# A quantised cross-attention and mixture-of-experts kernel on one core: a new instruction order for its front, and small jobs moved between VectorE, ScalarE and GpSimd

## The reference, cut to what matters

```python
# x (2, 512, 1024) f32, ctx_4096 (2, 1024, 1024) f32; all scales are 8/255, all zero points 128
def fake_quant(x, scale, zp):
    q = clip(round(x / scale + zp), 0, 255)
    return (q - zp) * scale

def xattn(x1, x2):                      # quantised product of normed tokens with the context
    return matmul(fake_quant(x1, s1, z1), fake_quant(x2, s2, z2))

def ffn(xt):                            # 1024 tokens
    scores = softmax(xt @ router_w + router_b) + router_bias
    # best 2 of 4 groups of experts, then best 2 of the 16 experts; their scores gate them
    for e in range(16):                 # here two experts are in use
        h = silu(xt @ ew1[e] + eb1[e]) * (xt @ ew2[e] + eb2[e])
        y += gate[:, e, None] * (h @ ew3[e] + eb3[e])
    z = silu(xt @ sw1 + sb1) * (xt @ sw2 + sb2) @ sw3 + sb3      # shared expert, 512 wide
    return y + z

x = x + tanh(g_xattn) * xattn(layernorm(x), ctx_4096)
x = x + tanh(g_ffn) * ffn(layernorm(x))
```

## Time and profile before

| what | value |
|---|---|
| device time, 3 runs | 317.53, 317.70, 319.18 us; median 317.7 |
| the profiled execution | 317.24 us, of which the profiler's span is 315.4 us |
| TensorE busy | 302.6 us, 96% of the span |
| VectorE busy | 206.3 us, 65% |
| ScalarE busy | 115.0 us, 36% |
| GpSimd busy | 13.9 us, 4% |
| granted TensorE clock | 0.998 of full speed |

### The profile page before, as it was taken

One profiled execution on the slowest core, in us unless ns is written; L12 is line 12 of the kernel. 1 busy time (PEld: TensorE's weight loads), 2 busy tenths in 40 slices (PEclk: granted clock), 3 DMA queues, 4 the chain that ended last, 5 costly groups with the idle time before them and its releaser, 6 DMA issues.

```text
span 315.4 us, 4716 instructions
## 1 busy us (share of the span) xinstructions
PE 302.6 (96%) x1867; PEld 153.3 (49%) x1867; DVE 206.3 (65%) x346; ACT 115.0 (36%) x129; POOL 13.9 (4%) x27
## 2 busy tenths in 40 slices
PE   4899899999999999999999999999999999999993
PEld 4653499644444446444444444444444444444441
DVE  3888999999998967776464361748564306135543
ACT  2877689589633559211108000064000000111000
POOL 2100120100002110000000000000000000000000
PEclk9999999999999999999999999999999999999999
DMA  7999908447620547105800008400000000000355
GB/s 234 410 337 321 304 12 250 150 101 214 220 66 0 108 94 72 1 2 167 301 0 2 0 0 290 178 0 0 2 0 0 2 1 1 0 2 0 134 204 202
DMA packets 43543, 34.55 MB, mean 110 GB/s; under 512 B 24060, under 2 KB 38396, under 8 KB 43516
## 3 DMA queue, kind: packets, MB, share of 16 engines
q1 hardware_dynamic: 43508, 34.20, 35.6%
q10 hardware_dynamic: 8, 0.00, 0.0%
HBM read 26.86 MB, written 4.19 MB: 98 GB/s over the span
## 4 chain that ended last, share of the span: by engine, by line
PE 60%; DVE 25%; DMA 4%; ACT 4%; issue 3%; POOL 2%; POOLq 0%; ACTq 0%; DVEq 0%; SPq 0%
PE PS L1426 26%; PE PS L1233 13%; PE PS L1447 13%; PE PS L1274 7%; DVE stats L691 6%; DVE X L778 3%; DVE areaW L755 3%; POOL lnR L399 2%; DMA areaT<-ring 2%; ACT QI L450 1%; DMA ring<-in_L_ffn_sw_dram 1%; DVE S L742 1%; DVE X L1017 1%; DVE area L738 1%; DMA X<-in_x_dram 1%
## 5 line engine op out<-in xcount | busy, mean ns | idle before, releaser
L1233 PE MATMUL PS<-areaT,areaW 128*128 128x512 f16 x288 | 62.5, 379 | 0.0
L1233 PEld LDWEIGHTS PS<-areaT,areaW 128*128 128x128 f16 x288 | 28.0, 98 | 33.7
L1274 PE MATMUL PS<-SW,areaH 128*128 128x512 f16 x192 | 41.8, 379 | 0.0
L1447 PE MATMUL PS<-areaW,areaH 128*128 128x512 f16 x192 | 41.8, 379 | 0.0
L1426 PE MATMUL PS<-areaT,area 128*128 128x512 f16 x192 | 41.6, 379 | 0.0
L1426 PE MATMUL PS<-areaT,areaW 128*128 128x512 f16 x192 | 41.6, 379 | 0.0
L635 ACT ACTIVATE SA<-PS,ecol 128x512 f32<-128x512 f32 x8 | 5.5, 689 | 93.2 <-PE PS L1426 93.2
L1105 DVE SCALAR_TENSOR_TENSOR X<-PS,gcol,X 128x1024 f32<-128x1024 f32 (+1 forms) x18 | 21.0, 1165 | 15.8 <-PE PS L1447 15.8
L1076 DVE SCALAR_TENSOR_TENSOR SA<-PS,ecol,SA 128x512 f32<-128x512 f32 x8 | 6.0, 751 | 38.2 <-ACT SA L635 38.2
L1176 PE MATMUL PS<-area,areaQ 128*128 128x512 f16 x128 | 30.0, 379 | 0.9 <-DVE areaQ L721 0.3
L1274 PEld LDWEIGHTS PS<-SW,areaH 128*128 128x128 f16 x192 | 18.8, 98 | 22.6
(11 more groups left out here) (164 smaller groups left out, 308.8 us busy)
## 6 DMA issues: line engine op xcount, KB each, us to landing
areaT<-in_ctx_dram SPq DMA_DIRECT2D x12, 512.0 KB, 8.1
ring<-in_L_ffn_sw_dram SPq DMA_DIRECT2D x12, 512.0 KB, 5.4
X<-in_x_dram SPq DMA_DIRECT2D x8, 512.0 KB, 5.9
ring<-in_L_ffn_ew_dram SPq DMA_DIRECT2D x4, 1024.0 KB, 7.2
out_dram<-X SPq DMA_DIRECT2D x7, 512.0 KB, 2.6
ring<-in_ctx_dram SPq DMA_DIRECT2D x4, 512.0 KB, 3.8
wrow<-in_L_ffn_ew_dram SPq DMA_DIRECT2D x2, 1024.0 KB, 9.6
rows<-in_L_ffn_eb_dram SPq DMA_DIRECT2D x2, 512.0 KB, 9.5
```

Of the source, the lines that this page charges most:

```text
L1233: last = mm(PS[:, SU_BANK[half * SC + c] + w, lo:hi], SW[:, wp, 2 * c + w, k, :], XT[:, xp, k, tk], start=(k == 0 and n == 0), stop=(k == ...
L1274: last = mm(PS[:, pb + h, :], HT[:, hp, c, i * P:(i + 1) * P], SW3[:, wp, c, hs], start=(c == 0 and n == 0), stop=(c == SC - 1 and n == 2))
L1447: last = mm(PS[:, 2 * (i % 2) + h, :], HE[:, hp, c, i * P:(i + 1) * P], W3S[j][:, wp, c, hs], start=(c == 0 and n == 0), stop=(c == HC - 1 ...
```

## The change

Eight edits, in the order of the diff below:

1. The first loads come in another order: context chunk 0 ahead of tile 1, chunks 2 to 4 ahead of tile 3.
2. ScalarE copies all four turned tiles (`evac_q1(0..3)`), VectorE none; chunk 0 is quantised ahead of tile 0.
3. VectorE's order: the chunk sums `add_s2` are taken apart from the clamps and put at other places; `attend(0)` and `bn(0)` stand ahead of five of the six small coefficient operations, and `coefs(0)` ahead of `attend(1)`.
4. TensorE's order in the front: `idle_products` after the first are 14 and 30 in place of 14, 18, 10 and 26, and `products(2, 6)` comes ahead of the column sums; of tile 3, seven chunks in place of five precede `transpose_high(0)`.
5. `open_block` is gone; the first matmul of `first_high(0, 0, c)` in each bank carries `start=True`.
6. `add_columns` for tiles 5 to 7 is done by GpSimd, before `attend` of the tile in place of after it; tile 4 stays on VectorE.
7. `token_sum` of tiles 6 and 7 and `row_terms(1)` come after the loop over tiles 4 to 7, ahead of `ln2_lo(7)`.
8. SyncE issues the `SB3` load behind the four `turn_tokens`.

```diff
             load_x(0)
...
+            load_ctx0(0)
             load_x(1)
-            load_ctx0(0)
             load_ctx0(1)
-            load_ctx0(2)
             load_x(2)
+            for k in range(2, 5):
+                load_ctx0(k)
             load_x(3)
-            for k in range(3, KC):
+            for k in range(5, KC):
                 load_ctx0(k)
...
+            for i in range(TB, NT):
+                turn_tokens(i)
             sp.wait_ge(rs_rdy, TB)
             sp.dma_start(SB3, sb3.partition_broadcast(P)).then_inc(sb3_in, 16)
-            for i in range(TB, NT):
-                turn_tokens(i)
...
+            def add_columns(i):
+
+                nc.gpsimd.tensor_tensor(X[:, i, :], X[:, i, :], RC[:, :], ALU.add).then_inc(col_add, 1)
+
+            pool.wait_ge(rc_rdy, 1)
+            pool.wait_ge(x_int, NT)
             for i in range(TB, NT):
+                if i + 1 < NT:
+                    add_columns(i + 1)
                 rstd(i, 1, 2 * TB + i + 1)
...
-            quant_x(0)
             act.wait_ge(tanh_rdy, 1)
             quant_ctx(0, 0)
+            quant_x(0)
             quant_ctx(0, 1)
+            evac_q1(0)
+            quant_ctx(0, 2)
             quant_x(1)
-            quant_ctx(0, 2)
+            quant_x(2)
             evac_q1(1)
             quant_ctx(0, 3)
-            quant_x(2)
+            evac_q1(2)
             quant_ctx(0, 4)
-            evac_q1(2)
+            quant_ctx(0, 5)
             quant_x(3)
-            quant_ctx(0, 5)
+            quant_ctx(0, 6)
             gate_tanh()
-            quant_ctx(0, 6)
             quant_ctx(0, 7)
+            evac_q1(3)
...
             clamp_x(0)
+            clamp_only(0)
+            dve.wait_ge(x_in[2], 16)
+            bn(2)
+            coefs(1, 1, cf[:, 3:4], None, sc6[:, 1:2])
+            clamp_only(1)
...
+            coefs(2, 1, cf[:, 3:4], None, sc6[:, 1:2])
+            clamp_only(2)
+            clamp_x(1)
+            add_s2(1)
+            clamp_x(2)
+            dve.wait_ge(x_in[3], 16)
+            bn(3)
+            clamp_only(3)
+            add_s2(2)
+            add_s2(3)
+            coefs(3, 1, cf[:, 3:4], None, sc6[:, 1:2])
+            clamp_only(4)
...
+            add_s2(4)
+            clamp_only(5)
...
+            clamp_x(3)
+            add_s2(5)
+            clamp_only(6)
+            add_s2(6)
+            clamp_only(7)
+            add_s2(7)
             dve.wait_ge(tanh_rdy, 2)
             link(v.tensor_scalar(cf[:, 4:5], cf[:, 0:1], sc6[:, 0:1], sc6[:, 2:3], ALU.mult, ALU.mult))
+            attend(0)
+            bn(0)
+            link(v.tensor_scalar(cf[:, 9:10], sc6[:, 3:4], -1.0, HALF, ALU.mult, ALU.add))
             link(v.tensor_scalar(cf[:, 7:8], cf[:, 4:5], cf[:, 9:10], None, ALU.mult))
             link(v.tensor_scalar(cf[:, 5:6], cf[:, 4:5], cf[:, 8:9], None, ALU.mult))
+            coefs(0, 1, None, XS, None)
             link(v.tensor_scalar(cf[:, 6:7], cf[:, 7:8], cf[:, 8:9], float(D), ALU.mult, ALU.mult))
             link(v.tensor_scalar(cf[:, 11:12], cf[:, 1:2], 1.0 / DNS, None, ALU.mult))
-            attend(0)
-            bn(0)
             attend(1)
-            coefs(0, 1, None, XS, None)
             bn(1)
...
-            token_sum(TB + 2)
-            token_sum(TB + 3)
-            row_terms(1)
             small_work()
...
             for i in range(TB, NT):
+                if i > TB:
+                    dve.wait_ge(col_add, i - TB)
                 attend(i)
-                add_columns(i)
+                if i == TB:
+                    add_columns(i)
                 bn(i)
                 if i > TB:
                     ln2_lo(i - 1)
                 coefs(i, 1, None, XS, None)
+            token_sum(TB + 2)
+            token_sum(TB + 3)
+            row_terms(1)
             ln2_lo(NT - 1)
...
-            def open_block(c):
-
-                pe.wait_ge(at_read, c + 2)
-                for w in range(2):
-                    mm(PS[:, 4 + 2 * c + w, :], zeroh[:, :], Q2[:, 0, 0:S], start=True, stop=False)
...
             idle_products(14)
             pe.wait_ge(q1_rdy, 1)
-            for k in range(2):
-                pe.wait_ge(q2_rdy, k + 1)
-                products(0, k)
+            pe.wait_ge(q2_rdy, 1)
+            products(0, 0)
+            idle_products(30)
             transpose_q1(1)
-            idle_products(18)
+            pe.wait_ge(q2_rdy, 2)
+            products(0, 1)
+            pe.wait_ge(q2_rdy, 3)
+            products(0, 2)
+            transpose_q1(2)
             pe.wait_ge(q1_rdy, 2)
             products(1, 0)
             products(1, 1)
-            idle_products(10)
...
             column_sums(1)
-            products(2, KC - 2)
             products(2, KC - 1)
             column_sums(2)
             pe.wait_ge(q1_rdy, TB)
-            for k in range(5):
+            for k in range(KC - 1):
                 products(TB - 1, k)
             transpose_high(0)
-            for k in range(5, KC):
-                products(TB - 1, k)
+            products(TB - 1, KC - 1)
             column_sums(TB - 1)
```

More of the change, by code:

```diff
@@ L183, in build @@
         at_done, at_read = sem("at_done"), sem("at_read")
-        cs_done, rc_rdy = sem("cs_done"), sem("rc_rdy")
+        cs_done, rc_rdy, col_add = sem("cs_done"), sem("rc_rdy"), sem("col_add")
         ln_xs, ln_hi, ln_lo = sem("ln_xs"), sem("ln_hi"), sem("ln_lo")
@@ L716, in clamp_x @@
                 v.tensor_scalar(QB[:, i % 2, :], QI[:, 2 + i % 2, :], QMAX, -HALF, ALU.min, ALU.add).then_inc(x_q, 1)
-            def evac_q1(i):
-                dve.wait_ge(q1_T, i + 1)
-                v.tensor_copy(Q1T[:, i, :, :], bank16(2 + i % 2)).then_inc(q1_rdy, 1)
             def clamp_only(k):
@@ L730, in add_s2 @@
                 dve.wait_ge(q2_rdy, k + 1)
-                link(v.tensor_tensor(S2[:, :], S2[:, :], Q2[:, k, :], ALU.add))
+                ins = v.tensor_tensor(S2[:, :], Q2[:, 0, :] if k == 1 else S2[:, :], Q2[:, k, :], ALU.add)
+                if k == KC - 1:
+                    ins.then_inc(s2_rdy, 1)
+                else:
+                    link(ins)
             def clamp_ctx(b, k):
@@ L903, in _ @@
             dve.wait_ge(sc_rdy, 1)
+            v.reciprocal(cf[:, 2:3], sc6[:, 2:3])
+            v.tensor_copy(cf[:, 12:13], sc6[:, 3:4]).then_inc(tanh_rdy, 1)
             link(v.reciprocal(cf[:, 3:4], sc6[:, 0:1]))
             coefs(0, 1, cf[:, 3:4], None, sc6[:, 1:2])
-            link(v.reciprocal(cf[:, 2:3], sc6[:, 2:3]))
-            v.tensor_copy(cf[:, 12:13], sc6[:, 3:4]).then_inc(tanh_rdy, 1)
             dve.wait_ge(x_in[1], 16)
@@ L912, in _ @@
             clamp_x(0)
+            clamp_only(0)
[3 more added lines that the diff above has]
+            clamp_only(1)
+            dve.wait_ge(sg_T, 1)
+            v.tensor_copy(sc6[:, 4:6], PS[:, 3, 20:22]).then_inc(sc_rdy, 1)
+            coefs(2, 1, cf[:, 3:4], None, sc6[:, 1:2])
[10 more added lines that the diff above has]
+            clamp_only(4)
             link(v.tensor_scalar(cf[:, 8:9], sc6[:, 1:2], -1.0, HALF, ALU.mult, ALU.add))
@@ L927, in _ @@
                 .then_inc(c1_rdy, 1)
[L928 to L936, removed]
-            clamp_x(3)
[L938 to L942, removed]
+            clamp_x(3)
+            add_s2(5)
[3 more added lines that the diff above has]
+            add_s2(7)
             dve.wait_ge(tanh_rdy, 2)
             link(v.tensor_scalar(cf[:, 4:5], cf[:, 0:1], sc6[:, 0:1], sc6[:, 2:3], ALU.mult, ALU.mult))
+            attend(0)
+            bn(0)
+            link(v.tensor_scalar(cf[:, 9:10], sc6[:, 3:4], -1.0, HALF, ALU.mult, ALU.add))
             link(v.tensor_scalar(cf[:, 7:8], cf[:, 4:5], cf[:, 9:10], None, ALU.mult))
             link(v.tensor_scalar(cf[:, 5:6], cf[:, 4:5], cf[:, 8:9], None, ALU.mult))
+            coefs(0, 1, None, XS, None)
             link(v.tensor_scalar(cf[:, 6:7], cf[:, 7:8], cf[:, 8:9], float(D), ALU.mult, ALU.mult))
             link(v.tensor_scalar(cf[:, 11:12], cf[:, 1:2], 1.0 / DNS, None, ALU.mult))
-            attend(0)
-            bn(0)
             attend(1)
-            coefs(0, 1, None, XS, None)
             bn(1)
@@ L1241, in first_high @@
                 pe.wait_ge((tk_hi, tk_lo)[xp], i + 1)
+                if i == 0 and xp == 0:
+                    pe.wait_ge(at_read, c + 2)
                 for w in range(2):
@@ L1245, in first_high @@
                     for k in range(KC):
-                        mm(PS[:, 4 + 2 * c + w, tk], SW[:, 0, 2 * c + w, k, :], XT[:, xp, k, tk], start=False, stop=False)
-            def open_block(c):
-                pe.wait_ge(at_read, c + 2)
-                for w in range(2):
-                    mm(PS[:, 4 + 2 * c + w, :], zeroh[:, :], Q2[:, 0, 0:S], start=True, stop=False)
+                        mm(PS[:, 4 + 2 * c + w, tk], SW[:, 0, 2 * c + w, k, :], XT[:, xp, k, tk],
+                           start=(i == 0 and xp == 0 and k == 0), stop=False)
             def first_low():
@@ L1301, in _ @@
```

(19 more changed lines are left out.)

4 lines of the change are left out of this document (removed).

## The result

| kernel | device time, median (lowest to highest) | ratio to before |
|---|---|---|
| before, 6 runs | 317.62 us (317.13 to 319.18) | |
| changed, 6 runs | 320.34 us (319.63 to 322.58) | 1.0105, 95% interval 1.0083 to 1.0128 |

What follows compares the result with a forecast made beforehand. The prediction took TensorE, busy 96%, as the bound, released by the front, with VectorE's loop close behind. Gains of 1.4+0.2 = 1.6 us made 315.6 for the profiled execution and 316.2 for the median, range 315.4 to 317.8.

Steps and rivals of the forecast that it cites:

- The front up to `attend(0)`: Front, replayed with trace durations: `column_sums(0)` starts at 26.2, `attend(0)` at 27.25, which is 2.5 us earlier.
- Rival 2: Front: the new order stalls on ScalarE, two misses put `attend(0)` at 28.5 or later; gain 0.4, 317.3 us; chance 0.27.
- `attend(0)` to `transpose_low(2)`: VectorE without gaps: `attend(0)` and `attend(1)` 4.4 apart, TensorE waits for `ln2_lo`, `transpose_low(2)` starts at 47.6, 1.4 us earlier.
- the step that costs the zero products at nothing: TensorE ahead of `transpose_low(2)`: removing the zero products (0.86 us) gains nothing by itself, hidden in the wait for VectorE.
- `token_sum` and `row_terms` behind the loop: VectorE before `attend(4)`: moving them away counts 1.0 of 2.6 us, beside the front's 1.3; free to 0.1 behind `coefs(7)`.
- GpSimd's adds: Loop over tiles 4 to 7: 2.3 us per add, saves VectorE 3.8, delays `add_columns(4)` 1.6; `ln2_lo(7)` ends at 113.7.
- Rival 1: Loop over tiles 4 to 7: GpSimd's add too slow, nothing gained at 4.6 us, slower beyond 0.5% from 5.2; chance 0.05.
- The turn of tile 7 at 4.75: Ahead of the router: the DMA that turns tile 7 takes 4.75 us behind `ln2_lo(7)`.
- The slack: Ahead of the router: `ln2_lo(7)` ends at 113.7 and may end at 117.0, so 3.3 us to spare.
- The clock: TensorE's clock, now granted in full, was expected to stay so, with a fall only as a rival.
- rival 4: At `transpose_low(0)`: a 1.8 us wait and fewer idle matmuls drop the clock to 1.2 GHz, 2.7 us lost, 318.8; chance 0.04.
- the forecast 315.6: Profiled execution: 1.4 us from the front and 0.2 at the router off 317.24 give 315.6 us.

Runs made afterwards that it cites:

- E3: The changed kernel with 32 small idle matmuls ahead of TensorE's wait for turned tile 7 at the router; 319.32 us, ratio 1.0061.
- E4: The changed kernel with the `SB3` load issued only when the four turned tiles have landed; 321.29 us, ratio 1.0137.
- E5: The kernel before with edits 1 to 5 alone; 317.28 us, ratio 1.0018.
- E1: The changed kernel with `add_columns` of tiles 5 to 7 back on VectorE, after `attend`; 317.47 us, ratio 1.0007.
- E2: The changed kernel, adds still on GpSimd, single-tile `lnB` made by a `tensor_scalar` with one SBUF tensor and `lnA` as per-partition scalar; 316.62 us, ratio 0.9976.
- E7: E2 with 30 idle matmuls on zeros ahead of the wait at `transpose_low(0)`; 316.29 us, ratio 0.9971.
- E8: The changed kernel with `SB3` and the four expert bias loads issued only when the turned tiles have landed; 321.49 us, ratio 1.0116.
- E10: The changed kernel as it is, profiled once more; 322.17 us.
- E9: E7 with the loads back in the order of the kernel before (edit 1 undone); 317.96 us, ratio 1.0023.
- E6: The kernel before with edits 6 to 8 alone; 317.46 us, ratio 1.0009.
- E11: The kernel before as it is, profiled once more; 316.87 us.

## Why the prediction was wrong, by its own steps

1. **The front up to `attend(0)`: right where the loads come early.** 26.28 for 26.2, 27.43 for 27.25. But of nine profiles with the new order of the loads, four have `column_sums(0)` at 26.3 to 26.6 (the changed kernel's first, E3, E4, E5), and five at 27.3 to 27.8 (E1, E2, E7, E8, E10). E9, with the old order, has 28.29, and E6 and E11 have the old front. So the 26.28 is partly luck: the forecast put tile 1's landing at 8.6, and in the first profile `bn(1)` starts at 7.87. In E10 it starts at 8.43, still earlier than forecast, and `column_sums(0)` is at 27.70. ScalarE's wait of 0.90 at `evac_q1(1)` is what the replay didn't have. Rival 2 named this place and its price and got 0.27; it is there in about half of the profiled executions.
2. **`attend(0)` to `transpose_low(2)`: right to 0.3.** The distance of the `attend`s is 4.46 for 4.4; the waits are 1.72 and 0.68 for 1.8 and 0.9; the gain is 1.14 for 1.4. TensorE waits for VectorE at both places, as the step that costs the zero products at nothing said; taking them out alone was not tried.
3. **`token_sum` and `row_terms` behind the loop: about right.** `attend(4)` starts at 88.76, 2.0 earlier than before, where 2.3 was forecast.
4. **GpSimd's adds: the size right, the consequence wrong. This is the step that failed.** The add took 2.35 for 2.3, and it held `add_columns(4)` up by 1.34 for 1.6. But "Behind the add on GpSimd stands the power of the tile before [...] so it isn't late" looked only at GpSimd. I did not go through the VectorE instructions that fall inside the add. One of them is `lnB`, and it is not chance: the power releases both the add and `coefs`. Two times 1.95 us make 3.9, and 113.7+0.3-0.3+3.9 = 117.6 is the 117.70 that was measured (the 0.3 are those of step 3 and of `add_columns(4)`). Rival 1 had the right victim and the wrong trigger: it let the loop become the bound only for an add of 4.1 us or more. The adds are 2.35 long and the loop is the bound all the same. The Trainium skill's rule on the shared port ("SBUF — State Buffer", who interferes with whom) says just this, and the traces agree: 2.11 with two SBUF inputs, 0.21 with one. The forecast used the rule for the 1024-column add and forgot the one-column operations, though the rule knows no size.
5. **The turn of tile 7 at 4.75: 1.1 too short.** It took 4.2 to 6.1 in the thirteen profiles, and 5.89 in the first of the changed kernel. The slack would have covered that, had step 4 held, as E2 shows. The slack itself was 2.9 us and not 3.3: 118.19 less the 0.2 of waiting and less 1.4 is 116.6, where the forecast had 117.0.
6. **The clock: right where the forecast looked, in part; blind at the router.** The forecast saw no wait at the router and so no fall of the clock there; it cost 1.7. At `transpose_low(0)`, where rival 4 had it at 0.04 for 2.7 us, it was at 0.86 for ten us in E1, E2 and E10, at 1.00 in the first profile of the changed kernel, in E3, E4, E5 and E8, and at 1.00 with the wait filled (E7). Ten us at 0.86 are 1.4 us of lost clock.

The sum of the deviations for the profiled execution: 0.38 (TensorE reaches the router 1.02 earlier and not 1.4), 1.87 (no wait was forecast, step 4 with step 5) and 1.7 (clock behind it) make 3.95 of the 4.03 us between 315.6 and 319.63.

Step 4 accounts for the sign, not for the whole miss. With `lnB` repaired (E2) the median gains 0.5 us and not 1.5. Two of its five executions, 315.72 and 315.79, come near the forecast 315.6; steps 1 and 6 are what the profiles show against the others.

**What stays open.** Why the turn of tile 7 takes 5.4 to 6.1 us in E1, E2, E3, E4, E5, E8, E10 and the changed kernel, and 4.2 to 4.8 in E6, E7, E9, E11 and the kernel before. E2 and E7 differ in 30 idle matmuls in the front only. E4 and E8 exclude the loads behind it, E5, with 5.36, shows a turn longer than that of the kernel before without edits 6 to 8. Nor is it shown what makes tile 1's load late in half of the profiled executions, or why the same wait of 1.7 to 1.8 us at `transpose_low(0)` is followed by the low clock in some and not in others. The three with the low clock all have the late front (27.57 to 27.78), but E8 has it too, at 27.67, and keeps the full clock. The forecast's other suspects, the idle matmuls and the four copies on ScalarE, were not tried alone.

## What to carry to other kernels

When work goes to GpSimd, list every VectorE instruction that can start inside it and count its SBUF inputs, tiny ones above all: here a one-column operation waited for the rest of the add as a thousand-column one did (1.95 and 1.34 us), and all that stood behind it waited too. Where such a pair is fixed by a semaphore, it meets every time; giving the small operation one tensor and a per-partition scalar took it out of the conflict (0.21 us beside the add). And a wait of TensorE can have two prices, itself and the clock behind it (1.7 and 1.7 us at this router), so slack there was worth more than its own length.

## What the runs showed of the hardware that I had not expected

- A 128x1 VectorE operation with two SBUF inputs took 2.11 us beside a GpSimd add of 2.34, and 0.16 without; with one SBUF tensor and a per-partition scalar it took 0.21 beside the same add.
- The clock fell to the 1.2 GHz level behind the same wait of 1.72 us in some executions of a kernel only, and once (E6) with TensorE idle for about 0.1 us, behind small router matmuls.
- The same DMA of one turned tile took 4.2 to 6.1 us from profile to profile, and 5.99 with nothing issued behind it.
- Two executions of one kernel differed by 0.56 us in the landing of a load issued at 2.21 us, and by 1.42 us 20 us later.
